# Moving the down-projection loads and the output stores of a fused state-space and ternary-FFN layer to each other's DMA queue

## The reference

```
delta = softplus(LN(x) @ Wd.T + bd)
state[d,n] = exp(-delta * a[d,n]) * state[d,n] + delta * b[d,n] * LN(x)[d]   # scan over 2048 steps
y = sum_n state[d,n];  x = x + LN(y @ Wo.T + bo)                             # 1024 channels, 16 states
h  = silu(bitlinear(LN(x), w_gate)) * bitlinear(LN(x), w_up)                 # 1024 -> 4096
x  = x + LN(bitlinear(h, w_down))                                            # 4096 -> 1024
```

## Time and profile before

| | us |
|---|---|
| median of 3 runs | 3987.54 (3986.54 to 3991.01) |
| profiled execution, whole | 3986.49 |
| its span, slowest core (core 0) | 3985.0 |
| spans of the other cores | 3969.2 to 3981.6 |

### The profile page before, as it was taken

How to read it: one execution, slowest core, us unless ns; L and a number is a source line. 1 busy time by engine, 2 the same in 40 slices (tenths; PEclk the granted TensorE clock), 3 DMA queues, 4 the chain that set the end, 5 groups by cost and what they waited for, 6 DMA issues and landing times.

```text
span 3985.0 us, 25422 instructions; the slowest of 8 cores (3969.2 to 3985.0 us)
## 1 busy us (share of the span) xinstructions
PE 1226.3 (31%) x5181; PEld 519.4 (13%) x5260; DVE 1502.7 (38%) x2048; ACT 1435.4 (36%) x2046; POOL 348.0 (9%) x543
## 2 busy tenths in 40 slices
PE   1121111100022221237310252652542735518453
PEld 0000000000000010113100010221111312103221
DVE  0005656569910002004678402266512477032500
ACT  2653535333356564652233104233123223132201
POOL 0001221123300000001112200000000000000000
PEclk9965555655555555558655676775776866759676
DMA  4052212100043431433100111220120300113011
GB/s 68 0 169 95 74 64 105 21 11 0 0 147 107 143 100 42 127 116 106 32 1 0 32 49 57 74 74 0 53 74 20 106 23 32 53 42 116 32 48 48
DMA packets 113146, 245.36 MB, mean 62 GB/s; under 512 B 6113, under 2 KB 71906, under 8 KB 108898
## 3 DMA queue, kind: packets, MB, share of 16 engines
q1 hardware_dynamic: 92770, 176.35, 13.4%
q0 software_dynamic: 20224, 67.38, 6.1%
HBM read 218.80 MB, written 33.55 MB: 63 GB/s over the span
## 4 chain that ended last, share of the span: by engine, by line
DVE 26%; PE 24%; ACT 18%; DMA 16%; issue 11%; POOL 3%; DVEq 1%; ACTq 1%; POOLq 0%; SPq 0%
DVE s_sig L291 10%; PE pD L1055 9%; DMA s_td<-tdT 6%; PE pU L936 5%; PE pG L928 4%; DVE s_ytmp L315 4%; DVE s_sig L298 4%; POOL s_state L265 3%; PE ptD L1014 2%; ACT s_h L1021 2%; DVE s_qs L963 2%; DMA tgT<-wg_stage 2%; PE pW L726 1%; DMA tdT<-wdn_stage 1%; DMA tuT<-wu_stage 1%
## 5 line engine op out<-in xcount | busy, mean ns | idle before, releaser
L284 ACT ACTIVATE s_abar<-s_dyq,s_nega 128x512 f32<-128x512 bf16 x512 | 369.4, 722 | 632.2 <-DVE s_sig L291 487.1
L291 DVE TENSOR_TENSOR_SCAN s_sig<-s_abar,s_state,s_lnf 128x512 bf16<-128x512 f32 x384 | 493.0, 1284 | 103.7 <-ACT s_abar L284 64.1
L1055 PE MATMUL pD<-s_td,s_h 128*128 128x512 bf16 x1000 | 338.1, 509 | 497.7 <-DMA s_td<-tdT 490.4
L928 PE MATMUL pG<-s_tg,s_dyq 128*128 128x512 bf16 x980 | 380.3, 388 | 85.1 <-DVE s_h L958 83.9
L936 PE MATMUL pU<-s_tu,s_dyq 128*128 128x512 bf16 x1024 | 397.2, 388 | 24.8 <-DMA s_tu<-tuT 18.6
L315 DVE SCALAR_TENSOR_TENSOR s_ytmp<-s_sig,s_bprm,s_ytmp 128x512 bf16<-128x512 bf16 x448 | 336.5, 751 | 47.9 <-DVE s_sig L291 0.9
L265 POOL TENSOR_TENSOR s_state<-s_sig,s_onesp 128x1 bf16<-128x1 bf16 x384 | 248.2, 646 | 853.6 <-DVE s_sig L291 553.2
L958 DVE TENSOR_TENSOR s_h<-s_gtmp,pU 128x512 bf16<-128x512 bf16 x128 | 88.1, 688 | 510.4 <-ACT s_gtmp L950 510.4
L1055 PEld LDWEIGHTS pD<-s_td,s_h 128*128 128x128 bf16 x1024 | 123.5, 125 | 711.4 <-issue 669.6
L950 ACT ACTIVATE s_gtmp<-pG,s_r1g 128x512 bf16<-128x512 f32 x128 | 87.9, 687 | 341.0 <-PE pU L936 190.6
L1085 DVE TENSOR_SCALAR s_nt<-s_st 128x4 f32<-128x4 f32 x4 | 0.7, 170 | 531.0 <-ACT s_h L1080 531.0
(11 more groups left out here) (172 smaller groups left out, 1796.5 us busy)
## 6 DMA issues: line engine op xcount, KB each, us to landing
wg_b<-wg SPq DMA_DIRECT2D x32, 1024.0 KB, 6.0
wu_b<-wu SPq DMA_DIRECT2D x32, 1024.0 KB, 5.4
wdn_b<-wdn SPq DMA_DIRECT2D x32, 1024.0 KB, 5.6
s_tg<-tgT SPq DMA_DIRECT2D x64, 512.0 KB, 3.5
s_tu<-tuT SPq DMA_DIRECT2D x64, 512.0 KB, 4.9
s_td<-tdT POOLq DMA_DIRECT2D x64, 512.0 KB, 4.0
tgT<-wg_stage POOLq DMA_DIRECT2D x16, 512.0 KB, 3.8
tuT<-wu_stage POOLq DMA_DIRECT2D x16, 512.0 KB, 3.8
```

What stands on the lines that cost most here:

```text
L284: lambda h, d=dc, n_=n, p=pa: h.activation(out=s_abar[:, p, :], in_=delta_view[:, d, t0:t0 + QT], func=AF.Exp, scale=s_nega[:, d, n_:n_ + 1]),
L291: lambda h, d=dc, c_=col, p=pa, s=ps: h.tensor_tensor_scan(s_sig[:, s, :], s_abar[:, p, :], lnT_view[:, d, t0:t0 + QT], s_state[:, c_:c_ + 1],
L928: h.matmul(pGs[c_][:], q1T_view[:, k, t_ * 128:(t_ + 1) * 128], s_tg[:, wp, k4_, :], start=(k == 0), stop=(k == KC - 1)),
L1055: lambda h, c_=c, k=kc, p=par, s_=sub, f=hf: h.matmul(pDs[c_][:, f * 512:(f + 1) * 512], q2T_view[:, c_, k, :], s_td[:, p, s_, f * 512:(f ...
```

## The change

The loads of `s_td`, 64 in all, move from the POOL queue to the SP queue, and the 16 stores to `out` move from the SP queue to the POOL queue. The waits that each of them carries stay as they were, and so do its size, its buffer and its semaphore.

```diff
@@ -1027,7 +1027,7 @@
                 for q in range(2):
                     w_dma = [prev_t_dn] if g > 0 else []
-                    sch.dma("gpsimd", f"td{q}",
+                    sch.dma("sync", f"td{q}",
                             lambda h, q_=q: h.dma_start(out=s_td[:, q_, :, :],
                                                         in_=tdT_v[:, q_, :, :]),
                             waits=w_dma)
@@ -1040,7 +1040,7 @@
                         if q >= 2:
-                            sch.dma("gpsimd", f"td{par}",
+                            sch.dma("sync", f"td{par}",
                                     lambda h, q_=q, p=par: h.dma_start(
                                         out=s_td[:, p, :, :], in_=tdT_v[:, q_, :, :]),
                                     waits=[ST("tensor")])
@@ -1138,7 +1138,7 @@
                     t_o = ST("vector")
-                    sch.dma("sync", "out0",
+                    sch.dma("gpsimd", "out0",
                             lambda h, t_=tc: h.dma_start(out=out_r[:, t_, :],
                                                          in_=s_out[:]),
                             waits=[t_o])
```

## The result

The changed kernel takes 3826.4 us, the median of 8 runs (3817.02 to 3831.25); the kernel before took 3986.8 us in 8 runs beside them. The ratio is 0.9594, 95% interval 0.9583 to 0.9606: 4.1% or 162 us faster. The forecast was 3829. The profiled execution took 3819.83 us, its span is 3818.3 us, and the slowest core is now core 4; the cores spread over 3793.4 to 3818.3, wider than the 3969.2 to 3985.0 of before; the clock rival, further down, comes back to this.

What follows compares the result with a forecast made beforehand. No engine bounds the whole; in group 0 the down-projection loads wait on POOL's queue behind the scan work's copies. 3986.5 - 165.3 - 10 + 16.6 = 3827.8, plus 1.05 for the median: 3829 us, range 3812 to 3843.

Steps and rivals of the forecast that it cites:

- the clock rival: Down projection, groups 1 to 3: shorter pauses keep the clock up, bursts take 3.6 us; in full 3717 us; chance 0.22.
- Part 1: Group 0: loads leave the queue behind the scan work's copies, PE starts about 2027, L1067 follows the last exponential; -165.3 us.
- Part 2: Down projection, groups 1 to 3: 42 pauses each 0.98 us shorter, a quarter of 41.2 us arrives; -10 us.
- Part 3: Stores to `out` through POOL: slower reaction and landing, 13 stores count at 1.28 us each; +16.6 us.
- Part 4: What is passed on the queues: next group's weight loads issued some 40 us earlier, no copies behind the stores; zero.
- The rival that nothing changes: Whole kernel: changing the queue changes nothing, only parts 2 and 3 are left, 3994, or 3987 with neither; chance 0.03.
- The slower rival: Group 0: scan work and matmuls hinder each other; rounds growing 1.65 us lose the gain, 2 us gives 4021; chance 0.02.

Runs made afterwards that it cites:

- the part alone: One part each against the kernel before: group 0's loads on SP 0.9601; loads of groups 1 to 3 on SP 0.9985; stores on POOL 1.0031.
- half loads: Each down-projection load cut in two 256 KB halves with a semaphore each, against the kernel with all loads and stores on SP: 3681.56 us, 0.9245 to the kernel before.
- wait for the pair before last: Load of pair q waits for pair q-2, not q-1, against the kernel with all loads and stores on SP: 3551.42 us, 0.8919 to the kernel before.

## Why the prediction was right, and where it was only nearly so

**What bounds the kernel.** Right. The single wait of 221.7 us was the queue's order: it goes when group 0's loads leave POOL (ratio 0.9601), and only changes sides when the order on POOL is reversed.

**Part 1, -165.3 us.** Measured 164.0 at L1067 on core 4 and 159 for the part alone. The stage started at 2028 (forecast 2027). L1067 stood behind ACT's last exponential, not behind PE or DVE, as said. The slack of some 55 us held: PE's first group stage takes 152.9 us, ends at 2181 and costs nothing.

**Part 2, -10 us.** SP's reaction is 0.08 us and the landing 3.6 for the assumed 3.5. The pause was forecast at 3.65 us; it is 3.67 in the round shown, but 3.92 in the mean of the 56 waits, a gain of 0.76 (core 4) to 0.88 (the two pages) for the 0.98 forecast. A quarter of 41 us was let through; the part alone measured 2 to 9 us, so even that was a little much. The reason given was that a burst which starts sooner is in the slow part of the clock for longer. The bursts of 6.4 us at 0.67 to 0.71 agree with it; when within a burst the clock rises, and why, no run isolates.

**Part 3, +16.6 us.** Mechanism right, one term too large. POOL's reaction cost 0.5 us as worked out, but the landing only 0.2 (2.9 for 2.7) where 0.8 was taken. The nearest row, `tgT` at 3.8 us on the same queue, takes 0.9 us more than the store does there, so that part of its time is not the queue's; that it comes from its shorter pieces is likely and not shown. The measured cost is 8 to 16 us for the part alone and 10.5 by the trace. ACT's 12 waits were to grow by about 15 us and grew from 53.5 to 59.7 (from 50.5 on core 4).

**Part 4, zero.** Right for the weight loads: in group 1 the first four were issued from 2172.02 on, right behind the last `s_td` load, and PE's waits for `s_tu` did not grow: three of 19.5 us in all before, two of 18.7 now. In both, nearly all of it is one wait at the very start of group 0 (18.6 and 18.0 us), which the change does not touch; the rest is 0.9 and 0.7. The two loads at L1031 do collide with the weight loads that they now follow: they land in 6.2 to 7.7 us, for 4.0 to 4.6 before, but long before PE needs them.

**The sum.** 3829 against 3826.4 is closer than the terms: the gain of part 1 was 1 to 6 us too large, that of part 2 some 4, and the cost of part 3 some 5 too large, which takes it back. That is luck. The range of 3812 to 3843 has a slip too: with the ends that it names its low end is 3829 + 10 - 16.6 - 24 + 7 = 3805, not 3812.

**The clock rival**, given 0.22, did not come about on the slowest core, and the runs show how near it was. Group 3 in the changed kernel, core 4 and then core 5 (landings of group 3 on core 4, of all groups on core 5; then ACT's wait for the stage), which answer to the earlier trace rows:

```profile
DMA to landing us min/median/max: 3.5/3.6/4.0
3771.45 4.73 ACT L1067 ACTIVATE s_dyq<-pD,s_r2d 128x1024 bf16<-128x1024 f32 x4 [150.66 <-PE pD L1055]
```

```profile
DMA to landing us min/median/max: 3.3/3.5/7.5
3746.60 4.74 ACT L1067 ACTIVATE s_dyq<-pD,s_r2d 128x1024 bf16<-128x1024 f32 x4 [141.56 <-PE pD L1055]
```

Core 5 lands its loads a little sooner and is through the stage 9.1 us sooner, 0.65 us a round. It is not alone (median landing of all groups; ACT's wait for the stage of group 3):

| core | landing, us | ACT's wait, us |
|---|---|---|
| 0 | 3.6 | 150.4 |
| 1 | 3.4 | 147.0 |
| 2 | 3.6 | 153.4 |
| 3 | 3.4 | 141.5 |
| 4 | 3.6 | 150.7 |
| 5 | 3.5 | 141.6 |
| 6 | 3.6 | 148.5 |
| 7 | 3.4 | 141.7 |

Over groups 1 to 3 the stage takes 145.0 us in the mean on cores 1, 3, 5 and 7, at a mean pause of 3.71 us, and 150.9 on cores 0, 2, 4 and 6, at 3.86: 0.15 us a round less in the pause goes with 0.42 less in the round. In the kernel before the same four cores lead by 0.20 us a round, 4.56 for 4.76, and it brings nothing: 152.9 and 152.8 us. That goes with the wider spread of the cores. So the rival did come about in part on half of the cores. The time of the kernel stayed with the slow ones.

**The rival that nothing changes** is refuted: 3987 by the rule, 3826.4 measured. The sentence of the Trainium skill beside it in the prediction ("DMA: Bandwidth & Descriptors", section "Issuing engines are not separate DMA queues"), that several issuing engines save only the time to initiate a DMA, is not the whole cost here. The transfers agree with it nearly: by the queue a load lands 0.4 us sooner and a store 0.2 later. What it leaves out is what stands ahead on the issuing queue, 216 us for the loads of group 0 (2026.81 to 2243.12). **The slower rival**, scan rounds stretched by matmuls beside them, is refuted: the rounds of group 0 still follow each other in 2.24 us, and this row has 184 DVE instructions at 184.82 / 184 = 1.004 us, for 1.004 in the earlier trace rows:

```profile
2028.00:2235.00 207.00, 184.82 (x184) 61.02 (x92) 0.64 0.14 46
```

## What to carry to other kernels

When an engine waits for a DMA far longer than the DMA takes, look at the queue that issued it: ask what stood ahead of it and which engine that waited for. Reversing two blocks on one in-order queue only moved the wait here; a second queue removed it. Then look at what the load itself waits for. Here half of a double buffer went unused, and one token index (0.8919 together with the queue) was worth more than the queue.

## What the runs showed that was not expected

The time of a stage of bursts and pauses is not linear in the pause. A stage here is a first burst of 32 matmuls and 14 rounds of a pause and 16 matmuls. The table has the means over groups 1 to 3, from PE's timeline of every core; the length runs from the first matmul to the end of the last, and the clock is that of the stretches shown:

| kernel | cores | mean pause, us | stage, us | granted clock |
|---|---|---|---|---|
| before | all | 4.66 | 152.8 (151.0 to 155.4) | 0.76 (group 1) |
| changed | 0, 2, 4, 6 | 3.86 | 150.9 (147.9 to 153.6) | 0.67 to 0.71 |
| changed | 1, 3, 5, 7 | 3.71 | 145.0 (141.2 to 149.5) | |
| half loads | all | 2.83 | 107.0 (102.8 to 113.3) | 0.85 |
| wait for the pair before last | all | 0.23 | 62.5 (60.5 to 65.3) | 0.95 |

From the first row to the second the 14 pauses are 11 us shorter and the stage 2; from the second to the third 2 and 6; from the third to the fourth 12 and 38. So a shorter pause was worth almost nothing down to 3.9 us, and three times its length from there to 2.8. The kernels of the last two rows differ from the others in how the loads are cut and in what the DMA does beside the bursts, so that the pause alone makes these numbers is the likeliest reading and not isolated.
